# Feed-forward attention, last two head quads: scores of the fourth made beside the third's softmax, output projections spread between the two chains

## Chip, cores and metric

One Trainium2 chip, one core of it. The metric is the device time of one execution in microseconds (us). Shown are three plain executions and one profiled one.

## What is computed

A cross attention over 16 sequences of 128 rows is added to `x`; then a routed feed-forward layer works on the 256 rows (of 2048) that a router picks. Only that second layer is touched by the change:

```python
h = _rms_norm(x, ln1_w)                      # 256 picked rows x 512
q = (h @ wq + bq).reshape(S, 16, 128)        # rope is applied to q and kk
kk, v = ...                                  # 8 heads each, repeated to 16
att = softmax(where(causal, q.kk / sqrt(128), -max))
x1 = x + (att @ v).reshape(S, 2048) @ wo
h2 = _rms_norm(x1, ln2_w)
processed = x1 + silu(h2 @ w_gate) * (h2 @ w_up) @ w_down
gate = sigmoid(sel_scores)
output = hidden.at[picked].set(gate * processed + (1 - gate) * x)
```

## The kernel before

Every engine runs a program of its own, in the order in which it is written; semaphores tie them together. All matrix products are made of three passes (`product`): each operand is split into a high part, rounded to the matmul's fp32 format, and the rest, and high x high, high x low and low x high are added up in PSUM. So whatever PE is to multiply is first copied by ACT (the `_hi` copy) and then subtracted by DVE (the `_lo` part). For weights, ACT makes `wp_hi` (`split_high`) and POOL makes `wp_lo` (`split_low`, line 849); a weight piece is 512x512, and four slots hold pieces in turn (`wp_hi[n % NSLOT]`). Piece `n` may be split only when piece `n-4` has been used: `split_high` waits for `used_up[n - NSLOT]`. The pieces in question are 9, 10 and 11 (rows of `wo` for quads 1, 2, 3, in slots 1, 2, 3), 13 (`w_up`, first piece, slot 1) and 14 (`w_gate`, second piece, slot 2; in the code `P_MLP + 2`).

The 256 picked rows are two blocks of 128 (`j`). The 16 heads are four quads (`n`, `FQ = 4`) of four heads. For one quad the stages are: `turn_queries` (eight transposes of the roped queries), their hi and lo copies, `score_quad` (PE, three PSUM tiles), mask and maximum (DVE, lines 1581 and 1587), `Exp` head by head (ACT, line 1144), reciprocal (DVE, line 1595), normalisation (POOL, line 885), `turn_probs` (PE, 12 transposes, lines 1954 to 1959), hi and lo copies of the probabilities `fp`, `mix_quad` (PE, probabilities times values), hi and lo copies of the mixed heads `foT`, and `attend_out` (PE, products with a piece of `wo`, added up over all quads in the banks `b_xT` and `b_scores`' second half; per block j and quad it is 12 matmuls). `attn_done` counts finished groups of `attend_out`.

Up to quad 2 the query projections of the next quad stand between these stages on PE. For the last quad there are none left. PE's program from quad 2 on is written by hand:

```python
turn_queries(3); turn_probs(2); mix_quad(2); score_quad(3); attend_out(2)
turn_probs(3); mix_quad(3); attend_out(3)
```

with `attend_out(1)` just ahead of it, behind `score_quad(2)`. After that DVE adds the attention to the picked rows (`add_attention`, line 1610), ACT squares and sums the rows (`row_squares`, line 1044), POOL takes the inverse root (`row_rsqrt`, lines 855 and 858), DVE weighs the rows (`weigh`, line 1431), PE turns them (`turn_h`) and the MLP begins with `gate_rows(0, 0)`. On ACT `split_high(P_MLP + 2)` stands ahead of `row_squares`, and on POOL `split_low(P_MLP + 2)` stands ahead of `row_rsqrt`.

Two more steps matter. DVE forms the router's dot products `g_dot` (line 1603, both inputs in SBUF) between the reciprocals of quad 3 and the lo parts of its probabilities; the sigmoid from it (`g_exp` on ACT, line 1166; `g_one` and `gate` on DVE, lines 1619 and 1621) stands just ahead of the MLP's first `silu` step (line 1627).

Of the kernel before, what the change touches and what calls it, by code (L numbers as in the profile page):

```python
# [5 lines left out]
def xattn_then_routed_ffn(  # L6
# [48 lines left out]
    P = 128  # L55
# [89 lines left out]
    with ctx:  # L145
# [101 lines left out]
        with ExitStack() as st:  # L247
# [32 lines left out]
            f_max = sb_in(st, "f_max", [P, 8])  # L280
            f_sum = sb_in(st, "f_sum", [P, 8])
            f_inv = sb_in(st, "f_inv", [P, 8])
# [8 lines left out]
        base = [by_cos, by_sin]  # L291

# [13 lines left out]
        f_W = [b_xT, b_s2]  # L306

# [400 lines left out]
        def _(pool):  # L708
# [168 lines left out]

            for n in range(FQ):
# [4 lines left out]
                for i, (heads, col) in enumerate(SCORE_TILES):  # L883
                    pool.wait_ge(f_inverted, 3 * n + i + 1)
                    pool.tensor_tensor(
                        fs[i][:].rearrange("p (h t) -> p h t", h=heads),
                        fs[i][:].rearrange("p (h t) -> p h t", h=heads),
                        f_inv[:, col:col + heads].unsqueeze(2).to_broadcast([P, heads, W // heads]),
                        ALU.mult).then_inc(f_normed, 1)
# [22 lines left out]
        def _(act):  # L912
# [194 lines left out]
            def probs_high(n):  # L1107

                act.wait_ge(fp_turned, 3 * n + 1)
                wait(act, f_mixed, 2 * n)  # L1110
                copy(fp0_hi[:, 0:2, :].rearrange("p h t -> p (h t)"), f_T[:]).then_inc(fp_hi_done, 1)
                act.wait_ge(fp_turned, 3 * n + 2)
                copy(fp0_hi[:, 2:4, :].rearrange("p h t -> p (h t)"), f_T2[:]).then_inc(fp_hi_done, 1)
                act.wait_ge(fp_turned, 3 * n + 3)
                copy(fp1_hi[:].rearrange("p h t -> p (h t)"), f_S[:]).then_inc(fp_hi_done, 1)

            def mixed_high(n):
                for g in range(2):
                    act.wait_ge(f_mixed, 2 * n + g + 1)

                    wait(act, attn_done, NJ * n)
                    copy(foT_hi[:, 2 * g:2 * g + 2, :].rearrange("p h t -> p (h t)"),
                         (f_O, f_T)[g][:]).then_inc(fo_hi_done, 1)

            for n in range(FQ):
                for j in range(NJ):
# [3 lines left out]
                    copy(fqT_hi[:, j].rearrange("p h t -> p (h t)"), (f_T, f_T2)[j][:]  # L1130
                         ).then_inc(fq_hi_done, 1)
                if n > 0:
                    probs_high(n - 1)
                if n < FQ - 1:
                    split_high(split_early(n))
# [4 lines left out]
                for i, (heads, col) in enumerate(SCORE_TILES):  # L1140
                    width = W // heads
                    act.wait_ge(f_maxed, 3 * n + i + 1)
                    for h in range(heads):
                        e = act.activation(fs[i][:, h * width:(h + 1) * width],
                                           fs[i][:, h * width:(h + 1) * width], ACT.Exp,
                                           bias=f_max[:, col + h:col + h + 1],
                                           accum_out=f_sum[:, col + h:col + h + 1])
                    e.then_inc(f_exped, 1)
                if n == FQ - 1:
                    split_high(split_early(n))  # L1150
# [14 lines left out]
            act.wait_ge(g_dotted, NJ)  # L1165
            act.activation(g_exp[:], g_dot[:], ACT.Exp, scale=-1.0).then_inc(g_exped, 1)
# [17 lines left out]
        def _(dve):  # L1184
# [356 lines left out]

            def probs_low(n):
                for i, (hi, lo, bank) in enumerate((
                        (fp0_hi[:, 0:2, :], fp0_lo[:, 0:2, :], f_T),
                        (fp0_hi[:, 2:4, :], fp0_lo[:, 2:4, :], f_T2),
                        (fp1_hi[:], fp1_lo[:], f_S))):
                    dve.wait_ge(fp_hi_done, 3 * n + i + 1)
                    low(lo.rearrange("p h t -> p (h t)"), bank[:],
                        hi.rearrange("p h t -> p (h t)")).then_inc(fp_lo_done, 1)

            def mixed_low(n):
                for g in range(2):
                    dve.wait_ge(fo_hi_done, 2 * n + g + 1)
                    low(foT_lo[:, 2 * g:2 * g + 2, :].rearrange("p h t -> p (h t)"), (f_O, f_T)[g][:],
# [547 lines left out]
```

## Time and profile before

| what | us |
|---|---|
| median of 3 executions (873.81 to 878.23) | 876.07 |
| the profiled execution | 879.73 |
| its span, first to last instruction | 878.0 |
| PE busy / DVE busy / ACT busy / POOL busy | 820.9 / 577.5 / 474.0 / 464.0 |
| mean granted TensorE clock, as a share of full speed | 0.977 |

Busy time is an average over stages. The quads of the feed-forward attention run from about 717 to 796 us of the span, the MLP from 800 us to the end; what this change touches lies between 757 and 815 us. A row of the timeline gives the start, the duration, the engine, the line, the operation with output and inputs, and in brackets how long the engine sat idle before it and what released it. A matmul's duration includes its way through the array: back to back ones start every 0.23 us (512 columns) and overlap.

### The profile page before, as it was taken

To read this page: it belongs to the slowest core of one execution; us is meant where nothing else is said; L and a number is where in the kernel's file an instruction comes from. 1 tells how busy PE (TensorE), PEld (TensorE's weight loads), DVE (VectorE), ACT (ScalarE), POOL (GpSimd) and SP (SyncE) were. 2 spreads that over 40 slices of the span, in tenths; PEclk is the share of its full clock that TensorE was granted. 3 is DMA by queue.
4 is the path that set the end of the run, shared out by engine and by line. 5 is a ranking of instruction groups with operands and counts; after the bars stand their busy time and mean duration, and the time that the engine had idled before them with its cause. 6 is when DMAs were issued, how large, how long until landed. Compare 5 with 4: busy or idle time off the path is not lost. (4 is left out here: it accounts for less than half of the span.)

```text
span 878.0 us, 14307 instructions
## 1 busy us (share of the span) xinstructions
PE 820.9 (93%) x4216; PEld 683.7 (78%) x4216; DVE 577.5 (66%) x1049; ACT 474.0 (54%) x1620; POOL 464.0 (53%) x485
## 2 busy tenths in 40 slices
PE   6999958999999999999999999999987799978997
PEld 4888836888888888888888888888875677766786
DVE  4454445677777777777777777777677588663513
ACT  4555534565566566566566566566554256553431
POOL 2333324555555555555555555555557196644980
PEclk9999997999999999999999999999998699999999
DMA  6566654011111111111111111111024565303520
GB/s 206 202 203 204 202 180 135 13 61 36 48 60 36 48 60 36 48 60 36 48 60 36 48 60 36 48 60 36 24 90 140 213 182 178 118 29 117 192 97 24
DMA packets 49287, 81.37 MB, mean 93 GB/s; under 512 B 4144, under 2 KB 12464, under 8 KB 49264
## 3 DMA queue, kind: packets, MB, share of 16 engines
q1 hardware_dynamic: 48688, 79.25, 27.5%
q0 software_dynamic: 576, 1.84, 0.6%
q8 instruction: 12, 0.20, 0.1%
q14 instruction: 11, 0.09, 0.0%
HBM read 63.77 MB, written 17.30 MB: 92 GB/s over the span
## 5 line engine op out<-in xcount | busy, mean ns | idle before, releaser
L1002 ACT ACTIVATE sq_junk<-q_row 128x128 bf16<-128x128 f32 x256 | 76.0, 298 | 159.6 <-DVE q_row L1256 159.6
L849 POOL TENSOR_TENSOR wp_lo<-raw,wp_hi 128x2048 fp32r<-128x2048 f32 (+1 forms) x24 | 105.0, 4385 | 45.3 <-ACT wp_hi L914 45.2
L1010 ACT ACTIVATE p_row<-s_row,neg_max 128x128 f32<-128x128 f32 x256 | 99.9, 392 | 37.0 <-DVE neg_max L1277 36.4
L1656 PE MATMUL b_y<-wo_hi,oT_hi 128*128 128x512 f32 x256 | 107.1, 419 | 1.0 <-DVE oT_lo L1187 1.0
L1656 PE MATMUL b_q<-wq_hi,xT_hi 128*128 128x512 f32 x252 | 105.6, 419 | 2.2 <-DVE k_row L1210 2.2
L780 POOL TENSOR_TENSOR p_row<-p_row,p_inv 128x512 f32<-128x512 f32 x64 | 66.6, 1041 | 66.7 <-DVE p_inv L1286 66.7
L1658 PE MATMUL b_y<-wo_hi,oT_lo 128*128 128x512 f32 x256 | 101.7, 397 | 0.0
L1657 PE MATMUL b_y<-wo_lo,oT_hi 128*128 128x512 f32 x256 | 101.6, 397 | 0.0
L1658 PE MATMUL b_q<-wq_hi,xT_lo 128*128 128x512 f32 x252 | 99.7, 396 | 0.0
L1657 PE MATMUL b_q<-wq_lo,xT_hi 128*128 128x512 f32 x252 | 99.6, 395 | 0.0
L738 POOL TENSOR_TENSOR q_rs<-q_ss,eps_head 128x4 f32<-128x4 f32 x64 | 12.7, 199 | 153.8 <-ACT sq_junk L1002 153.8
L1256 DVE TENSOR_TENSOR q_row<-b_q,bq_row 128x512 f32<-128x512 f32 x63 | 43.6, 692 | 40.7 <-PE b_q L1658 40.6
L1743 PE MATMUL b_scores<-kT,qT_hi 128*128 128x256 f32 x256 | 64.8, 285 | 5.6 <-DVE qT_lo L1261 5.5
L776 POOL TENSOR_TENSOR q_nrm<-q_row,q_rs 128x512 f32<-128x512 f32 x64 | 66.6, 1040 | 6.1 <-POOL q_rs L740 2.2
L740 POOL TENSOR_TENSOR q_rs<-q_rs,half 128x4 f32<-128x4 f32 x64 | 64.9, 1013 | 5.0
L1744 PE MATMUL b_scores<-kT,qT_lo 128*128 128x256 f32 x256 | 64.8, 285 | 0.0
L914 ACT ACTIVATE wp_hi<-raw 128x2048 fp32r<-128x2048 f32 x24 | 45.9, 1915 | 30.6 <-PE b_y L1658 15.8
L1187 DVE TENSOR_TENSOR oT_lo<-b_o,oT_hi 128x512 fp32r<-128x512 f32 x64 | 43.7, 683 | 21.3 <-ACT oT_hi L914 20.0
L1658 PEld LDWEIGHTS b_y<-wo_hi,oT_lo 128*128 128x128 f32 x256 | 48.5, 189 | 11.8
L1743 PEld LDWEIGHTS b_scores<-kT,qT_hi 128*128 128x128 f32 x256 | 49.1, 192 | 10.3 <-DVE qT_lo L1261 6.8
L1267 DVE TENSOR_TENSOR s_row<-b_scores,mask 128x512 f32<-128x512 f32 x64 | 44.3, 692 | 19.0 <-PE b_scores L1744 19.0
L1658 PEld LDWEIGHTS b_q<-wq_hi,xT_lo 128*128 128x128 f32 x252 | 48.0, 191 | 11.0
(298 smaller groups left out, 2266.0 us busy)
## 6 DMA issues: line engine op xcount, KB each, us to landing
cx<-in_ctx_dram SPq DMA_DIRECT2D x16, 256.0 KB, 2.6
wq_raw<-in_L_xattn_Wq_dram SPq DMA_DIRECT2D x16, 256.0 KB, 2.8
wo_raw<-in_L_xattn_Wo_dram SPq DMA_DIRECT2D x16, 256.0 KB, 3.1
v_store<-v_out SPq DMA_DIRECT2D x16, 256.0 KB, 3.3
k_store<-k_out SPq DMA_DIRECT2D x16, 256.0 KB, 2.0
xr<-in_x_dram SPq DMA_DIRECT2D x16, 256.0 KB, 2.7
k_raw<-k_store SPq DMA_DIRECT2D x16, 256.0 KB, 2.6
v_raw<-v_store SPq DMA_DIRECT2D x16, 256.0 KB, 2.8
```

The costliest lines, as they stand in the source:

```text
L740: pool.tensor_tensor(dst, dst, half[:, 0:dst.shape[1]], ALU.pow).then_inc(rooted, 1)
L776: pool.tensor_tensor(q_nrm[:], q_row[:], per_head(q_rs, HD), ALU.mult).then_inc(q_normed, 1)
L780: pool.tensor_tensor(p_row[:], p_row[:], per_head(p_inv, S), ALU.mult).then_inc(p_normed, 1)
L849: pool.tensor_tensor(wp_lo[n % NSLOT][:, part, :], raw[RAW_OF[n]][:, part, :], wp_hi[n % NSLOT][:, part, :].bitcast(fp32), ALU.subtract).t ...
L914: return act.activation(dst, src, ACT.Copy)
L1002: sq = act.activation(sq_junk[:, h, :], q_row[:, h, :], ACT.Square, accum_out=q_ss[:, h:h + 1])
L1010: e = act.activation(p_row[:, h, :], s_row[:, h, :], ACT.Exp, bias=neg_max[:, h:h + 1], accum_out=p_sum[:, h:h + 1])
L1656: pe.matmul(dst, left[0], right[0], start=start, stop=False)
L1657: pe.matmul(dst, left[0], right[1], start=False, stop=False)
L1658: return pe.matmul(dst, left[1], right[0], start=False, stop=stop)
L1743: pe.matmul(b_scores[:, h, :], qT_hi[:, hs], keys, start=True, stop=False)
L1744: last = pe.matmul(b_scores[:, h, :], qT_lo[:, hs], keys, start=False, stop=True)
```

## The change

The scores of quad 3 are made on PE ahead of `turn_probs(2)`. To have room, quad 3 gets its own banks (`b_q`, `b_y`, `b_o` for queries and scores) and its own SBUF tiles for the scores (`proj[0]`, `proj[1]`, `by_cos` in place of `fs`), the statistics get two halves, and the mixed heads of quad 2 go into `hT` in place of `foT`. Since `by_cos` now holds scores, POOL's gather into it waits for the transposes of quad 3. The output projections are spread: block 0 of quad 1 ahead of the scores of quad 3, block 1 behind them; block 0 of quad 2 between the transposes and the mixing of quad 3; block 1 of quad 2 in two halves around block 0 of quad 3. The count that frees a weight slot follows that order. The sigmoid of the router moves ahead of the MLP on ACT and DVE.

```diff
+        def scores_of(n):
+            return (proj[0], proj[1], by_cos) if n == FQ - 1 else fs
+
+        def mixed_of(n):
...
+                     for t in (hT_hi, hT_lo)] if n == FQ - 2 else [foT_hi[:], foT_lo[:]]
...
+        def query_banks(n):
+            return (b_q, b_y) if n == FQ - 1 else (f_T, f_T2)
+
+        def score_banks(n):
+            return (b_q, b_y, f_O) if n == FQ - 1 else (f_S, f_T2, f_T)
+
+        def prob_banks(n):
+            return (b_q, b_y, f_S) if n == FQ - 1 else (f_T, f_T2, f_S)
...
+        OUTPUTS = [(n, j) for n in range(FQ - 2) for j in range(NJ)]
+        OUTPUTS += [(FQ - 2, 0), (FQ - 1, 0), (FQ - 2, 1), (FQ - 1, 1)]
+
+        def outputs_until(n, j):
+            return OUTPUTS.index((n, j)) + 1
...
-            used_up[p_wo(n)] = (attn_done, NJ * (n + 1))
+            used_up[p_wo(n)] = (attn_done, outputs_until(n, NJ - 1))
...
             pool.wait_ge(f_roped, NJ * (FK + FQ))
+            pool.wait_ge(fp_turned, 3 * FQ)
...
+            for n in range(FQ - 1):
+                queries_high(n)
...
+                if n == FQ - 2:
+                    queries_high(FQ - 1)
+                score_exps(n)
...
+            score_exps(FQ - 1)
+            probs_high(FQ - 2)
+            mixed_high(FQ - 2)
+            split_high(split_early(FQ - 1))
             probs_high(FQ - 1)
             mixed_high(FQ - 1)
+            act.wait_ge(g_dotted, NJ)
+            act.activation(g_exp[:], g_dot[:], ACT.Exp, scale=-1.0).then_inc(g_exped, 1)
             split_high(P_MLP + 2)
             for j in range(NJ):
                 act.wait_ge(x2_made, j + 1)
                 row_squares(NJ + j, x2_row[j][:])
+            act.wait_ge(attn_done, outputs_until(FQ - 2, NJ - 1))
...
+            mask_scores(FQ - 2, 0)
+            mask_scores(FQ - 2, 1)
+            queries_low(FQ - 1)
+            mask_scores(FQ - 2, 2)
+            invert(FQ - 2, 0)
+            invert(FQ - 2, 1)
+            mask_scores(FQ - 1, 0)
+            invert(FQ - 2, 2)
+            mask_scores(FQ - 1, 1)
+            mask_scores(FQ - 1, 2)
+            invert(FQ - 1, 0)
+            probs_low(FQ - 2)
+            invert(FQ - 1, 1)
+            invert(FQ - 1, 2)
+            mixed_low(FQ - 2)
...
             probs_low(FQ - 1)
             mixed_low(FQ - 1)
+            dve.wait_ge(g_exped, 1)
+            dve.tensor_scalar(g_one[:], g_exp[:], 1.0, None, ALU.add).then_inc(g_made, 1)
...
+            turn_queries(FQ - 1)
+            attend_out(FQ - 3, 0)
+            score_quad(FQ - 1)
+            attend_out(FQ - 3, 1)
+            turn_probs(FQ - 2)
+            mix_quad(FQ - 2)
             turn_probs(FQ - 1)
+            attend_out(FQ - 2, 0)
             mix_quad(FQ - 1)
-            attend_out(FQ - 1)
+            attend_out(FQ - 2, 1, range(0, 2))
+            attend_out(FQ - 1, 0)
+            attend_out(FQ - 2, 1, range(2, QUAD))
+            attend_out(FQ - 1, 1)
```

Three places in the built programs show it. First PE, from the transposes of the last queries to the last output projection; of every block its first instruction stands here (`wp_hi1`, `wp_hi2` and `wp_hi3` are the slots with `wo` for quads 1, 2 and 3). Before:

```order
L1663 MATMUL b_pT<-ident,turned1 128x128 [waits f_masked,f_roped]
L1954 MATMUL b_qT<-ident,fs0 128x128 [waits fq_lo_done,f_normed]
L1656 MATMUL b_o<-fp0_hi,fv_hi 128x512 [waits fo_lo_done,fp_lo_done]
L1656 MATMUL b_scores<-fkT_hi,fqT_hi 128x128 [waits fp_lo_done,fq_lo_done]
L1656 MATMUL b_xT<-wp_hi2,foT_hi 128x512 [waits fo_lo_done,piece_lo_pool]
L1954 MATMUL b_qT<-ident,fs0 128x128 [waits f_normed]
L1656 MATMUL b_xT<-wp_hi3,foT_hi 128x512 [waits fo_lo_done,piece_lo_pool]
```

and with the change:

```order
L1732 MATMUL b_y<-ident,turned1 128x128 [waits f_roped]
L1725 MATMUL b_xT<-wp_hi1,foT_hi 128x512 [waits fo_lo_done,piece_lo_pool]
L1725 MATMUL b_q<-fkT_hi,fqT_hi 128x128 [waits fq_lo_done]
L1725 MATMUL b_scores<-wp_hi1,foT_hi 128x512 [waits fo_lo_done,piece_lo_pool]
L2028 MATMUL b_qT<-ident,fs0 128x128 [waits fq_lo_done,f_normed]
L1725 MATMUL b_o<-fp0_hi,fv_hi 128x512 [waits fo_lo_done,f_masked,fp_lo_done]
L2028 MATMUL b_q<-ident,proj0 128x128 [waits fp_lo_done,f_normed]
L1725 MATMUL b_xT<-wp_hi2,hT_hi 128x512 [waits fo_lo_done,piece_lo_pool]
L1725 MATMUL b_scores<-wp_hi2,hT_hi 128x512 [waits fo_lo_done,piece_lo_pool]
L1725 MATMUL b_xT<-wp_hi3,foT_hi 128x512 [waits fo_lo_done,piece_lo_pool]
L1725 MATMUL b_scores<-wp_hi3,foT_hi 128x512 [waits fo_lo_done,piece_lo_pool]
```

The scores of quad 3 (`b_q<-fkT_hi`) now come ahead of the transposed probabilities of quad 2 (`b_qT<-ident,fs0`), and both blocks of `wo` for quad 2 (`wp_hi2`) come late; the second half of its block 1 is the last but one group of all.

Second ACT, from the split of piece 13 (`wp_hi1<-raw2`) to the first `row_squares` (`hn_row0,f_ss`); piece 14 is `wp_hi2<-raw0`. Before:

```order
L914 ACTIVATE wp_hi1<-raw2 128x2048 [waits attn_done,raw_loaded2]
L914 ACTIVATE fp0_hi<-b_qT 128x512 [waits f_mixed,fp_turned]
L914 ACTIVATE foT_hi<-b_qT 128x512 [waits attn_done,f_mixed]
L914 ACTIVATE wp_hi2<-raw0 128x2048 [waits attn_done,raw_loaded0]
L1044 ACTIVATE hn_row0,f_ss<-x2_row0 128x512 [waits x2_made]
```

and with the change:

```order
L941 ACTIVATE hT_hi<-b_qT 128x512 [waits f_mixed]
L941 ACTIVATE wp_hi1<-raw2 128x2048 [waits attn_done,raw_loaded2]
L941 ACTIVATE fp0_hi<-b_q 128x512 [waits f_mixed,fp_turned]
L941 ACTIVATE foT_hi<-b_qT 128x512 [waits attn_done,f_mixed]
L1196 ACTIVATE g_exp<-g_dot 128x2 [waits g_dotted]
L941 ACTIVATE wp_hi2<-raw0 128x2048 [waits attn_done,raw_loaded0]
L1071 ACTIVATE hn_row0,f_ss<-x2_row0 128x512 [waits x2_made]
```

The split of piece 13 has moved from behind the `Exp`s of quad 3 to behind the mixed heads of quad 2. The split of piece 14 stands where it stood, ahead of `row_squares`; what moved is the event that it waits for: `attn_done` was 6 (both blocks of quad 2, then ahead of quad 3's transposes) and is 7 now, which the second half of block 1 of quad 2 raises.

Third DVE, around the dot products `g_dot` (`fp0_lo`: lo parts of probabilities). Before:

```order
L1587 TENSOR_REDUCE f_max<-fs2 128x2 [waits f_masked]
L1595 RECIPROCAL f_inv<-f_sum 128x4 [waits f_exped]
L1595 RECIPROCAL f_inv<-f_sum 128x2 [waits f_exped] x2
L1603 ISA x2_row0,g_dot<-h_sel0,wr2_row 128x512 [waits f_rows_loaded]
L1603 ISA x2_row1,g_dot<-h_sel1,wr2_row 128x512
L1187 TENSOR_TENSOR fp0_lo<-b_qT,fp0_hi 128x512 [waits fp_hi_done]
```

and with the change:

```order
L1617 TENSOR_REDUCE f_max<-by_cos 128x2 [waits f_masked]
L1623 RECIPROCAL f_inv<-f_sum 128x4 [waits f_exped]
L1227 TENSOR_TENSOR fp0_lo<-b_qT,fp0_hi 128x512 [waits fp_hi_done]
L1623 RECIPROCAL f_inv<-f_sum 128x2 [waits f_exped] x2
L1227 TENSOR_TENSOR hT_lo<-b_qT,hT_hi 128x512 [waits fo_hi_done]
L1672 ISA x2_row0,g_dot<-h_sel0,wr2_row 128x512 [waits f_rows_loaded]
L1672 ISA x2_row1,g_dot<-h_sel1,wr2_row 128x512
L1227 TENSOR_TENSOR fp0_lo<-b_q,fp0_hi 128x512 [waits fp_hi_done]
```

Two reciprocals of quad 3 now stand behind the lo parts of quad 2's probabilities, and the dot products stand behind the mixed heads of quad 2.

## Rows read from the trace of the kernel before

**Rows 1.** Busy time by stretch: stretch, length, then PE, PEld, DVE, ACT, POOL busy (instructions), clock, DMA

```profile
757.90:760.70 2.80, 2.80 (x27) 2.80 (x26) 2.73 (x5) 2.40 (x2) 1.49 (x2) 1.00 0.07 16
777.10:782.60 5.50, 5.50 (x26) 4.31 (x24) 4.50 (x11) 5.35 (x17) 2.59 (x3) 1.00 0.00 0
815.00:860.00 45.00, 45.00 (x212) 37.50 (x211) 16.82 (x22) 18.28 (x19) 35.45 (x8) 1.00 0.40 140
```

**Rows 2.** Who PE waited for from 735 us on: total, times, longest

```profile
PE b_o L1656 <- DVE fp_lo L1187: 5.2, 4, 1.7
...
PE b_qT L1663 <- DVE hn_row L1431: 1.7, 1, 1.7
...
PE b_q L1656 <- DVE turned L1627: 0.9, 1, 0.9
```

**Rows 3.** The chain of work that ended last, pieces between 766 and 798 us

```profile
766.31 0.45 PE b_qT L1663 x4
...
769.52 0.61 ACT fp_hi L914
...
772.09 0.50 PE b_o L1656
...
789.71 1.91 ACT wp_hi L914
791.70 4.61 POOL wp_lo L849
...
797.26 0.75 DVE hn_row L1431
```

**Rows 4.** Timeline of PE: first matmul of quad 3's scores; turned rows; start of the MLP

```profile
774.31 0.22 PE L1656 MATMUL b_scores<-fkT_hi,fqT_hi 128*128 128x128 f32 x1
...
798.07 0.66 PE L1663 MATMUL b_qT<-ident,hn_row 128*128 128x128 f32 x4 [1.67 <-DVE hn_row L1431]
800.73 0.77 PE L1656 MATMUL b_q<-wp_hi,hT_hi 128*128 128x512 f32 x1 [2.00 <-DVE hT_lo L1187]
...
803.42 0.57 PE L1656 MATMUL b_q<-wp_hi,hT_hi 128*128 128x512 f32 x1
```

**Rows 5.** Timeline of DVE and ACT: mixed heads of quad 2, softmax of quad 3, piece 13

```profile
775.14 0.69 DVE L1187 TENSOR_TENSOR foT_lo<-b_qT,foT_hi 128x512 fp32r<-128x512 f32 x1 [0.36 <-ACT foT_hi L914]
777.12 0.68 DVE L1581 SCALAR_TENSOR_TENSOR fs<-b_pT,causal 128x512 f32<-128x512 f32 x1
778.45 0.68 DVE L1581 SCALAR_TENSOR_TENSOR fs<-b_qT,causal 128x512 f32<-128x512 f32 x1
...
774.51 0.60 ACT L914 ACTIVATE foT_hi<-b_qT 128x512 fp32r<-128x512 f32 x1 [0.45 <-PE b_qT L1658]
779.88 0.51 ACT L1144 ACTIVATE fs<-fs,f_max 128x256 f32<-128x256 f32 x1
780.88 1.90 ACT L914 ACTIVATE wp_hi<-raw 128x2048 fp32r<-128x2048 f32 x1
```

**Rows 6.** Timeline of POOL: normalisations of quads 2 and 3, and piece 13

```profile
765.17 3.03 POOL L885 TENSOR_TENSOR fs<-fs,f_inv 128x512 f32<-128x512 f32 x3
780.01 3.48 POOL L885 TENSOR_TENSOR fs<-fs,f_inv 128x512 f32<-128x512 f32 x3 [11.82 <-DVE f_inv L1595]
783.46 5.01 POOL L849 TENSOR_TENSOR wp_lo<-raw,wp_hi 128x2048 fp32r<-128x2048 f32 x1
```

**Rows 7.** Groups by line and shape: the two kinds of dot product: total us, mean ns

```profile
L1309 DVE CUSTOM_DVE_ANT_0 dot_junk<-h_row,wr_row 128x512 bf16<-128x512 f32 x16 | 11.1, 692 | 0.6
...
L1603 DVE CUSTOM_DVE_ANT_0 x_row<-h_sel,wr_row 128x512 f32<-128x512 f32 x2 | 3.0, 1510 | 0.0
```

**Rows 8.** Timeline of DVE at the MLP's first silu step

```profile
809.12 4.60 DVE L1619 TENSOR_SCALAR g_one<-g_exp 128x2 f32<-128x2 f32 x1 [2.17 <-ACT g_exp L1166]
```

**Rows 9.** Timeline of PE after two waits, an earlier place: first slow and first faster matmul

```profile
695.41 0.79 PE L1656 MATMUL b_y<-wp_hi,hT_hi 128*128 128x512 f32 x1 [2.28 <-DVE hT_lo L1187]
...
701.12 0.52 PE L1657 MATMUL b_scores<-wp_lo,hT_hi 128*128 128x512 f32 x1
```

More of the change, by code:

```diff
@@ L1105, in _, with queries_high @@
                     split_high(NSLOT + o)
[L1107 to L1125, printed above, removed]
+            def queries_high(n):
                 for j in range(NJ):
@@ L1129, in _, with probs_high, mixed_high, score_exps @@
                     wait(act, f_scored, 3 * n)
-                    copy(fqT_hi[:, j].rearrange("p h t -> p (h t)"), (f_T, f_T2)[j][:]
+                    copy(fqT_hi[:, j].rearrange("p h t -> p (h t)"), query_banks(n)[j][:]
                          ).then_inc(fq_hi_done, 1)
+            def probs_high(n):
+                places = (fp0_hi[:, 0:2, :], fp0_hi[:, 2:4, :], fp1_hi[:])
+                for i in range(3):
+                    act.wait_ge(fp_turned, 3 * n + i + 1)
+                    if i == 0:
+                        wait(act, f_mixed, 2 * n)
+                    copy(places[i].rearrange("p h t -> p (h t)"), prob_banks(n)[i][:]).then_inc(fp_hi_done, 1)
+            def mixed_high(n):
+                hi, lo = mixed_of(n)
+                for g in range(2):
+                    act.wait_ge(f_mixed, 2 * n + g + 1)
+                    if n == FQ - 1:
+                        act.wait_ge(attn_done, outputs_until(FQ - 3, NJ - 1))
+                    elif n < FQ - 2:
+                        wait(act, attn_done, NJ * n)
+                    copy(hi[:, 2 * g:2 * g + 2, :].rearrange("p h t -> p (h t)"),
+                         (f_O, f_T)[g][:]).then_inc(fo_hi_done, 1)
+            def score_exps(n):
+                for i, (heads, col) in enumerate(SCORE_TILES):
+                    width = W // heads
+                    tile_ = scores_of(n)[i]
+                    act.wait_ge(f_maxed, 3 * n + i + 1)
+                    for h in range(heads):
+                        e = act.activation(tile_[:, h * width:(h + 1) * width],
+                                           tile_[:, h * width:(h + 1) * width], ACT.Exp,
+                                           bias=f_max[:, n % 2, col + h:col + h + 1],
+                                           accum_out=f_sum[:, n % 2, col + h:col + h + 1])
+                    e.then_inc(f_exped, 1)
+            for n in range(FQ - 1):
+                queries_high(n)
                 if n > 0:
                     probs_high(n - 1)
-                if n < FQ - 1:
-                    split_high(split_early(n))
+                split_high(split_early(n))
                 if n > 0:
@@ L1139, in _ @@
                     split_high(piece)
[L1140 to L1150, printed above, removed]
+                if n == FQ - 2:
+                    queries_high(FQ - 1)
+                score_exps(n)
                 if n == 0:
@@ L1556, in mixed_low, with mask_scores @@
                         ).then_inc(fo_lo_done, 1)
-            for n in range(FQ):
-                if n < FQ - 1:
-                    o = PROJECTIONS.index(("q", n + 1))
+            def mask_scores(n, i):
+                heads, col = SCORE_TILES[i]
+                width = W // heads
+                tile_ = scores_of(n)[i][:].rearrange("p (h t) -> p h t", h=heads)
+                dve.wait_ge(f_scored, 3 * n + i + 1)
+                if n < FQ - 1:
+                    wait(dve, fp_turned, 3 * n)
+                dve.scalar_tensor_tensor(
+                    tile_, score_banks(n)[i][:].rearrange("p (h t) -> p h t", h=heads), SCALE,
+                    causal[:, 2 * P - width:2 * P].unsqueeze(1).to_broadcast([P, heads, width]),
+                    ALU.mult, ALU.add).then_inc(f_masked, 1)
+                dve.wait_ge(f_masked, 3 * n + i + 1)
+                dve.tensor_reduce(f_max[:, n % 2, col:col + heads], tile_,
+                                  AX.X, ALU.max, negate=True).then_inc(f_maxed, 1)
@@ L1561, in _, with invert @@
+            def invert(n, i):
+                heads, col = SCORE_TILES[i]
+                dve.wait_ge(f_exped, 3 * n + i + 1)
+                dve.reciprocal(f_inv[:, n % 2, col:col + heads],
+                               f_sum[:, n % 2, col:col + heads]).then_inc(f_inverted, 1)
+            for n in range(FQ - 2):
+                o = PROJECTIONS.index(("q", n + 1))
                 if n == 0:
                     take_rows(o, 0)
-                for j in range(NJ):
-                    dve.wait_ge(fq_hi_done, NJ * n + j + 1)
-                    low(fqT_lo[:, j].rearrange("p h t -> p (h t)"), (f_T, f_T2)[j][:],
-                        fqT_hi[:, j].rearrange("p h t -> p (h t)")).then_inc(fq_lo_done, 1)
@@ L1592, in _ @@
                     take_rows(PROJECTIONS.index(("v", 1)), 1)
-                for i, (heads, col) in enumerate(SCORE_TILES):
-                    dve.wait_ge(f_exped, 3 * n + i + 1)
-                    dve.reciprocal(f_inv[:, col:col + heads],
-                                   f_sum[:, col:col + heads]).then_inc(f_inverted, 1)
+                for i in range(3):
+                    invert(n, i)
                 if n == 0:
```

143 lines of the change are left out of this document (75 added, 68 removed).

## The prediction

> **What bounds the kernel now.** I read the view of who waited for whom first, on PE, since PE is the engine that is busy 93% of the span. From 735 us on it waits for little, and all of it lies at the end of the attention: 5.2 us in four waits for the lo parts of probabilities, and 1.7 us for the normalised row ahead of the MLP [rows 2]. The busy times by stretch show the same from the other side: in the scores of a quad (2.80 of 2.80 us) and in the output projection of a quad (5.50 of 5.50) PE has no gap, and none in the MLP from 815 to 860 us (45.00 of 45.00) [rows 1]. So a microsecond taken off the start of the MLP comes off the end of the kernel, and one added there is added.
>
> Then I read the chain that ended last, at the point where the MLP starts, because that tells what sets this start. It is not the last output projection. PE is done with it at 796.40 (798.07 less the 1.67 it then sat idle) [rows 4]. The chain goes through ACT's split of weight piece 14 at 789.71, POOL's lo part of it at 791.70 for 4.61 us, and only then the inverse root and the weighed row at 797.26 [rows 3]. POOL works in order, and this 4.61 us piece stands ahead of the inverse root. From the start of ACT's split to the turned row on PE it is 798.07 - 789.71 = **8.36 us**, whatever PE does meanwhile.
>
> **The change, part by part.** The work on PE is the same, 0 matmuls added or removed; what moves are its gaps. Up to the end of quad 2's scores at 760.70 nothing moves. From there I lay PE's new order out, on the clock of the profiled execution, with four transposes at 0.45 us [rows 3], a block of output projection at 5.50 / 2 = 2.75, scores at 2.80 [rows 1], and a mixing at 774.31 - 772.09 = 2.22 [rows 3, 4].
>
> - *First stretch, no gap.* Queries of quad 3 (0.9), block 0 of quad 1 (2.75), scores of quad 3 (2.80, done at 767.15), block 1 of quad 1 (2.75): 769.9. POOL has quad 2's probabilities normalised at 765.17 + 3.03 = 768.2 [rows 6]; DVE now puts the queries' two lo parts ahead of the last mask, and a mask of quad 3 ahead of the last reciprocal, some 2 us, but POOL is busy with piece 12 until 765.17 anyway, so I move this by at most 0.2. Transposes of quad 2 (1.35): 771.25.
> - *Quad 2's probabilities.* ACT's hi copies now stand behind all `Exp`s of quad 3. DVE takes the first mask of quad 3 at about 765.8 and the others 778.45 - 777.12 = 1.33 apart [rows 5], with one reciprocal between: the last maximum is there at 769.95. The last two `Exp`s take 780.88 - 779.88 = 1.0 [rows 5], so the copies start at 770.95. From that start to the mixing it is 772.09 - 769.52 = 2.57 [rows 3]: mixing at 773.5. PE sits idle 2.25, where it was idle 1.7.
> - *Quad 2 out.* Mixing until 775.75, transposes of quad 3 until 777.1 (two of its reciprocals stand behind quad 2's lo parts on DVE and are done at 773.5, POOL follows with two of the three tiles, 2.0 us, at 775.6: just in time). The mixed heads are ready 775.14 + 0.69 - 772.09 = 3.74 after a mixing starts [rows 3, 5], at 777.25. Block 0 of quad 2 until 780.05.
> - *Quad 3's probabilities.* The second hi copy of quad 2's mixed heads starts 774.51 - 772.09 = 2.42 into the mixing [rows 3, 5], at 775.9; ACT then splits piece 13, which used to lie behind quad 3's `Exp`s, 1.90 us [rows 5], until 778.3. The copies of quad 3 start there, and mixing 2.57 later at 780.9, if DVE is free by 778.9. It has the two dot products first, from 777.2 on.
> - *The dot products.* They took 1.51 us each; the same kind of product elsewhere took 0.69 [rows 7]. Beside them POOL's three normalisations took 3.48 in place of 3.03, and piece 13 took 5.01 [rows 6] in place of 4.61 [rows 3]: each lost about 0.45 while DVE lost 0.8. So they lengthened each other. Now they stand at 777.2 to 778.7, where POOL has nothing until ACT hands it piece 13 at 778.4. I take 0.73 each; with 1.51 each DVE would be free at 780.2 and mixing starts 1.2 us later. The Trainium skill, "SBUF — State Buffer", section "Who interferes with whom", says that a VectorE instruction with two SBUF inputs and a GpSimd instruction that reads SBUF exclude each other, the second waiting out the first; by it the sum would be the one with 0.73, by the row at face value 1.2 us more. The trace agrees: 1.51 is 0.69 and most of one 1.0 us normalisation.
> - *Quad 3 out.* Mixing 780.9 to 783.1, heads ready at 784.65. Half a block of quad 2 (1.38) fits in between. Block 0 of quad 3 until 787.4, the other half block until 788.8, block 1 of quad 3 until 791.5. PE is thus done **4.9 us earlier** than at 796.40.
> - *What takes it back.* ACT may split piece 14 only when slot 2 is free. That was long so when ACT came to it at 789.71 [rows 3]. Now ACT is free at 784.5, but the slot is used until the second half block of quad 2, 788.8, and the count rises some 0.2 after the next matmul could start: the split begins at 789.0. The piece on POOL and the inverse root stand behind it as before: 789.0 + 8.36 = 797.35 for the turned row, against 798.07. **Of 4.9 us, 0.7 are left.**
> - *The sigmoid.* DVE's `g_one`, two columns, took 4.60 us beside a POOL piece that began at the same moment [rows 8], and PE then waited 0.9 for the first `silu` step [rows 2]. Moved to about 785, where POOL only issues gathers, it stands on no path: **-0.9**.
> - *The clock.* PE will sit idle 797.35 - 791.7 = 5.7 us ahead of the turned row, then 2.0. Before it was 1.67 and 2.00, and the MLP started at half speed (1.2 GHz) for 803.42 - 800.73 = 2.7 us [rows 4]. After two longer idle times it was 701.12 - 695.41 = 5.7 us [rows 9]. In these 2.7 us six matmuls started, 0.45 each, against 5.50 / 24 = 0.23 [rows 1], so each microsecond at half speed costs about half of itself. Between 0 and 3.0 / 2 = 1.5; I take **+0.5**, since the idle stretch is longer and the place where speed comes back differs from one start to the next.
> - Wider statistics, other PSUM banks and other SBUF tiles are the same instructions with other addresses: nothing. POOL's extra wait ahead of its gathers ends at 777, while POOL is on piece 13 until 783: nothing; were it exposed, the gathers are needed only in the MLP.
>
> Sum: -0.7 - 0.9 + 0.5 = **-1.1 us** against 879.73, the profiled execution. That is 3.7 above the median; the same difference on the median of 876.07 gives **875.0**. Less than 0.5% (4.4 us) either way can't be told from no change here; the three executions alone spread over 4.4.
>
> **The rivals.**
> *The output projections set the start.* If piece 14 did not hold up the inverse root, the turned row would follow PE's last projection at 791.5 and the gain would be 6.6 + 0.9 = 7.5: about 868.5. For it: PE's order does end 4.9 us earlier. Against it: the order on ACT and POOL still has piece 14 first, and the count it waits for is raised by the last but one group.
> *The dot product meets piece 13 on POOL.* If the second dot product is issued after POOL has begun piece 13, DVE may stand until that ends, as `g_one` did for 4.60 us [rows 8]. The point is sharp: the dot product is issued at 777.95, the piece starts at 778.4, 0.45 us later, and both hang on the same copy of ACT. If it falls the other way, DVE is free at 778.4 + 4.61 + 0.55 = 783.55 in place of 778.9, mixing of quad 3 and all behind it is 4.6 later: -1.1 + 4.6 = +3.5, and with the clock at its upper bound +4.5: 879.6 to 880.6, slower than before.
> *The clock.* If the long idle time keeps the MLP's whole first two tiles slow, 24 matmuls at 0.22 more less the 6 slow ones of before, it costs 4.0 in place of 0.5: 878.5.
>
> **How the numbers follow.** The forecast, with what lies within a few microseconds of it, gets 0.62; the first rival, with any other way in which the early end of PE counts, 0.14; the dot product 0.10; the clock 0.10; the rest, spread, 0.04. The forecast's own bounds are -0.7 - 0.9 + 0 - 1 (links of the chain that are shorter than I laid them) = -2.6 and -0.7 + 1.2 - 0.9 + 1.5 = +1.1, so 873.5 to 877.2, with some 2 us for the median of few executions. To hold 8 of 10 the range must reach over the clock and towards the second rival: 871 to 880. Faster by over 0.5%: the first rival and a bit of scatter, 0.15. Slower by over 0.5%: the upper half of the second rival and the rest, 0.10. Within: 0.75.
>
> **What would show it.** Right: ACT's split of piece 14 starts right behind a wait for PE, near 789; POOL's piece follows it and the inverse root that; PE idles some 5 us ahead of the turned row; scores of quad 3 stand ahead of the transposes of quad 2 with no gap between; `g_one` takes well under 1 us; the dot products take 0.7 each. Wrong: the turned row comes close behind the last projection, or a dot product lasts over 4 us, or PE waits elsewhere in the MLP.

## The result: a little slower, and the profile after

| | before | after |
|---|---|---|
| median, us (20 runs each) | 878.16 (873.81 to 882.39) | 880.34 (876.77 to 883.25) |
| profiled execution: span, time, us | 878.0, 879.73 | 876.9, 878.74 |
| PE busy, us | 820.9 | 821.0 |

The ratio is **1.0028, 95% interval 1.0017 to 1.0039**: 0.0028 x 878 = 2.5 us slower, where the prediction had 1.1 faster. That is within the 0.5% either way to which the prediction gave 0.75, but it is clear of no change. Before is 2.1 us above the median that the prediction began with, so the differences are compared, not the times.

The profiled execution of after came to the first score of quad 2 at 753.81, 4.1 us earlier than that of before [rows 1]: the program up to there is the same, and single executions differ by that much (753.81 to 758.53 in the twelve traces of this document). So 4.1 is added to a time of after wherever it is compared with one of before ("aligned").

Busy time of PE by stretch in after (stretch, length, PE, PEld, DVE, ACT and POOL busy, clock, DMA share, GB/s), the scores of quad 2 and a place in the MLP:

```profile
753.80:756.60 2.80, 2.80 (x27) 2.80 (x26) 2.74 (x5) 2.40 (x2) 1.48 (x2) 1.00 0.15 19
...
829.20:833.60 4.40, 4.39 (x13) 3.49 (x14) 1.87 (x3) 0.00 (x0) 3.93 (x1) 0.63 0.64 233
```

The first row answers to the first of [rows 1] and is the same work at the same speed. The second lies where before had 45 us of MLP at a clock of 1.00 without a gap: now 4.4 us at 0.63, part of them at the lower of the two levels of the clock.

Who PE waited for from 735 us on, in after:

```profile
PE b_qT L1732 <- DVE hn_row L1471: 5.6, 1, 5.6
PE b_o L1725 <- DVE fp_lo L1227: 3.5, 3, 2.2
PE b_q L1725 <- DVE turned L1696: 2.7, 1, 2.7
PE b_q L1725 <- DVE hT_lo L1227: 1.6, 1, 1.6
```

Against [rows 2], the wait for the normalised row grew from 1.7 to 5.6, as forecast (5.7). The wait for `turned`, 0.9 before, was to go and is 2.7 now. It is not the same wait: before, it stood at the first `silu` step of the MLP; now there is none there, and 2.7 at the second. PE's timeline in after shows where:

```profile
769.41 0.50 PE L1725 MATMUL b_o<-fp_hi,fv_hi 128*128 128x512 f32 x1 [2.18 <-DVE fp_lo L1227]
776.67 0.50 PE L1725 MATMUL b_o<-fp_hi,fv_hi 128*128 128x512 f32 x1 [0.40 <-DVE fp_lo L1227]
...
793.29 1.11 PE L1732 MATMUL b_qT<-ident,hn_row 128*128 128x128 f32 x4 [5.64 <-DVE hn_row L1471]
795.97 0.76 PE L1725 MATMUL b_q<-wp_hi,hT_hi 128*128 128x512 f32 x1 [1.56 <-DVE hT_lo L1227]
...
829.21 0.47 PE L1725 MATMUL b_q<-wp_hi,hT_hi 128*128 128x512 f32 x1 [2.72 <-DVE turned L1696]
...
830.96 0.63 PE L1725 MATMUL b_q<-wp_hi,hT_hi 128*128 128x512 f32 x1
831.38 0.63 PE L1726 MATMUL b_q<-wp_lo,hT_hi 128*128 128x512 f32 x1
```

The turned row stands at 793.29 + 4.1 = 797.39 aligned (798.07 before, 797.35 forecast), the MLP at 800.07 against 800.73 [rows 4]. **Up to there the change gains 0.7 us, as forecast.** From the start of the MLP to the last step on DVE it is then 76.7 us, against 73.05 before: 3.7 lost. Less the 0.7, 3.0 in these two executions, near the 2.5 measured. The loss is in the row at 829.21: a gap of 2.72 us, and behind it matmuls that start 0.42 apart (half speed, 1.2 GHz) in place of 0.23, for some eight of them: about 1.6 us more. The first 12 matmuls of the MLP, partly at half speed too, took 0.3 us longer than before, and the wait of 0.9 at the first `silu` is gone: 2.7 + 1.6 + 0.3 - 0.9 = 3.7. The place lies behind the stretch of 757 to 815 us that the change was taken to touch.

The chain that ended last, in after, says what made PE wait:

```profile
785.02 1.93 ACT wp_hi L941
787.02 4.50 POOL wp_lo L872
...
792.48 0.75 DVE hn_row L1471
...
818.45 10.01 DVE h_sel L1712 x2
828.46 0.61 DVE turned L1696
829.21 0.47 PE b_q L1725
```

The upper rows are the piece 14 of [rows 3]. Below stands a step that the prediction never mentions: two instructions of VectorE on `h_sel` with 10.01 us between them. This is the **gating step**, `attn_row * gate + base`, two `scalar_tensor_tensor` with two big SBUF inputs each. It stands in the loop over the MLP at `m == 0`, ahead of the second `silu` step. VectorE in after, in order of time:

```profile
773.05 0.68 DVE L1672 CUSTOM_DVE_ANT_0 x_row<-h_sel,wr_row 128x512 f32<-128x512 f32 x1
...
780.33 0.16 DVE L1677 TENSOR_SCALAR g_one<-g_exp 128x2 f32<-128x2 f32 x1
...
818.45 5.03 DVE L1712 SCALAR_TENSOR_TENSOR h_sel<-h_sel,gate,by_cos 128x512 f32<-128x512 f32 x1
823.40 5.06 DVE L1712 SCALAR_TENSOR_TENSOR h_sel<-h_sel,gate,by_sin 128x512 f32<-128x512 f32 x1
828.38 0.68 DVE L1696 SCALAR_TENSOR_TENSOR turned<-proj,b_q 128x512 f32<-128x512 f32 x1
```

and the same step in before:

```profile
824.12 3.84 DVE L1643 SCALAR_TENSOR_TENSOR h_sel<-h_sel,gate,by_cos 128x512 f32<-128x512 f32 x1
827.88 0.74 DVE L1643 SCALAR_TENSOR_TENSOR h_sel<-h_sel,gate,by_sin 128x512 f32<-128x512 f32 x1
```

The second instruction took 0.74 us before and 5.06 after, on the same data. What changed is what POOL does at that moment. POOL in before:

```profile
809.08 18.33 POOL L849 TENSOR_TENSOR wp_lo<-raw,wp_hi 128x2048 fp32r<-128x2048 f32 x4 [8.79 <-ACT wp_hi L914]
828.81 4.63 POOL L849 TENSOR_TENSOR wp_lo<-raw,wp_hi 128x2048 fp32r<-128x2048 f32 x1 [1.40 <-ACT wp_hi L914]
```

and in after:

```profile
804.57 18.37 POOL L872 TENSOR_TENSOR wp_lo<-raw,wp_hi 128x2048 fp32r<-128x2048 f32 x4 [9.07 <-ACT wp_hi L941]
823.14 4.78 POOL L872 TENSOR_TENSOR wp_lo<-raw,wp_hi 128x2048 fp32r<-128x2048 f32 x1 [0.20 <-ACT wp_hi L941]
```

In both, the first gating instruction meets the fourth of four weight pieces that lie back to back, and ends 0.54 to 0.55 us after that piece does (827.96 against 827.41, 823.48 against 822.94). Before, POOL then had a gap of 1.40 us, and the second instruction ended at 828.62, **0.19 us before POOL's next piece**; it had begun 0.93 us before that piece (827.88 against 828.81). After, the gap is 0.20 us, the piece is there first (823.14 against 823.40), and the second instruction stands until the piece ends at 827.92.

The gap shrank because two chains moved against each other. POOL's next piece waits for ACT's split, and that for PE's up rows (this is ACT's row in before, then in after):

```profile
826.81 1.92 ACT L914 ACTIVATE wp_hi<-raw 128x2048 fp32r<-128x2048 f32 x1 [2.47 <-PE b_o L1658]
```

```profile
821.14 1.92 ACT L941 ACTIVATE wp_hi<-raw 128x2048 fp32r<-128x2048 f32 x1 [2.47 <-PE b_o L1727]
```

From the start of the MLP this is 26.08 us before and 25.17 after: 0.91 earlier, mostly the wait at the first `silu` (0.85) that the change removed. POOL's four pieces end 0.29 later (26.68 and 26.97), as they begin later behind the slower start of the MLP. 1.40 - 0.91 - 0.29 = 0.20: a shift of 1.20 us between the two chains, more than the 0.93 by which the second instruction had come first.

### The profile page after: what moved, and what is told of

The parts are those of the page before. It is cut to its first block and busy times, and to the rows that moved or that the text cites. A ratio compares the mean times of both kernels' runs of the same rounds, so it can differ in the third digit from the quotient of the medians.

```text
span 876.9 us, 14307 instructions
## 1 busy us (share of the span) xinstructions
PE 821.0 (94%) x4216; PEld 683.6 (78%) x4216; DVE 575.3 (66%) x1049; ACT 474.6 (54%) x1620; POOL 462.4 (53%) x485
## 5 line engine op out<-in xcount | busy, mean ns | idle before, releaser
L1725 PEld LDWEIGHTS b_q<-wq_hi,xT_hi 128*128 128x128 f32 x252 | 48.3, 192 | 10.5 <-issue 2.4
```

The source lines that it names most:

```text
L1725: pe.matmul(dst, left[0], right[0], start=start, stop=False)
```

## The experiments

The theory: the change gains what was forecast, and its early sigmoid brings the gating step to meet one GpSimd piece more, which costs more than all that was gained. The rival: the new order of the attention costs it, by its long idle time of PE, by the clock or otherwise. No run leaves out any of the computation. All ratios are to the kernel before; us are (ratio - 1) x 878; the last three columns are read from the traces.

| run | ratio, 95% interval | us | second gating instruction, us | POOL's gap, us | wait at the second `silu`, us |
|---|---|---|---|---|---|
| before | 1 | 0 | 0.74 | 1.40 | none |
| the change | 1.0028 (1.0017 to 1.0039) | +2.5 | 5.06 | 0.20 | 2.7 |
| change, gating late | 0.9979 (0.9957 to 1.0001) | -1.8 | 0.74 | 0.20 | none |
| change, gating early | 0.9995 (0.9972 to 1.0018) | -0.4 | 0.75 | 0.21 | none |
| change, sigmoid back | 0.9994 (0.9973 to 1.0016) | -0.5 | 0.74 | 1.43 | none |
| before, sigmoid early | 1.0031 (1.0011 to 1.0051) | +2.7 | 5.07 | 0.25 | 2.7 |
| before, gating late | 1.0005 (0.9983 to 1.0026) | +0.4 | 0.75 | 1.39 | none |
| before, sigmoid early, gating late | 0.9983 (0.9965 to 1.0001) | -1.5 | 0.74 | 0.26 | none |
| change, piece 14 late | 0.9968 (0.9952 to 0.9983) | -2.8 | 5.06 | 0.23 | 2.7 |
| change, piece 14 and gating late | 0.9918 (0.9897 to 0.9938) | -7.2 | 0.75 | 0.20 | none |
| before, piece 14 and gating late | 0.9989 (0.9973 to 1.0005) | -1.0 | 0.74 | 1.37 | none |
| change, both moves, and piece 14 behind the second weighing | 0.9916 (0.9886 to 0.9945) | -7.4 | 0.75 | 0.20 | none |

POOL's gap is 0.20 to 0.26 in every run with the early sigmoid and 1.37 to 1.43 in every run with the late one, whatever else differs. Only where the gating step stands at its old place does the second gating instruction meet that gap.

**The change, gating late.**

```diff
-                if m == 0:
+                if m == FI - 2:
```

> The changed kernel, with VectorE's gating step of the attention rows (the two scalar_tensor_tensor on h_sel, two SBUF inputs each) moved from the first silu step of the MLP to the last but one. Theory (the gating step now meets GpSimd's weight pieces, and PE waits for the silu behind it): the two gating instructions at their old place took 10.1 us and cost PE a wait of 2.7 us and 1.7 us of half speed; at the new place GpSimd has no piece left, they take about 0.75 us each, the wait and the half speed go, and the kernel is 4.4 us faster than the change: about 1.9 us faster than before, ratio 0.998. Rival (the new order of the attention, its long idle time of PE or its clock, costs the 2.5 us): the ratio stays 1.003, whatever the gating instructions take.

Measured: 0.9979, 0.0049 x 878 = 4.3 us under the change; its interval leaves out the rival's 1.003. The gating step and PE's waits in this run:

```profile
L1712 DVE SCALAR_TENSOR_TENSOR h_sel<-h_sel,gate,by_cos x1: 743/743/743, 855.6 to 855.6; 128x512 f32<-128x512 f32 x1
L1712 DVE SCALAR_TENSOR_TENSOR h_sel<-h_sel,gate,by_sin x1: 744/744/744, 856.3 to 856.3; 128x512 f32<-128x512 f32 x1
```

```profile
PE b_qT L1732 <- DVE hn_row L1471: 5.6, 1, 5.6
PE b_o L1725 <- DVE fp_lo L1227: 3.9, 3, 2.2
PE b_q L1725 <- DVE hT_lo L1227: 1.6, 1, 1.6
```

The wait of 5.6 us ahead of the turned row is all there, so it is not what makes the change slower than before; the wait of 2.7 is gone.

**Before, gating late**, the same edit on the kernel before, as a control.

> The kernel before, with the gating step moved to the last but one silu step, as a control. Theory: the gating instructions took 3.84 and 0.74 us there and no PE wait came of it, so 0 us, ratio 0.999 to 1.001. Rival (the late place is worth several microseconds by itself, whatever the change did, for instance since it frees GpSimd's weight pieces): 1 us faster or more, ratio below 0.9985; then the run of the change with the late gating does not speak for the theory.

Measured: 1.0005. The interval (0.9983 to 1.0026) shows no gain from the late place by itself, where no wait of PE came of the gating step.

**The change, gating early.** The whole gating step stands behind the second `h_low`, ahead of the loop, its waits with it:

```diff
             h_low(NJ + 1)
+            dve.wait_ge(attn_copied, NJ)
+            dve.wait_ge(g_made, 2)
+            dve.wait_ge(gathered_base, 16 * NJ)
+            for j in range(NJ):
+                dve.scalar_tensor_tensor(attn_row[j][:], attn_row[j][:], gate[:, j:j + 1], base[j][:],
...
```

> The changed kernel with the gating step not later but earlier: on VectorE right behind the second h_low, ahead of the first silu step of the MLP, where GpSimd has been idle since the inverse roots and takes its next piece only about 8.6 us after the start of the MLP. Theory (what costs is meeting a GpSimd piece, not the place in the MLP): both gating instructions take about 0.75 us, end some 0.4 us ahead of GpSimd's piece, the wait of 2.7 us goes: as with the gating late, 4.4 us faster than the change, ratio to before 0.998. Rival (it is the distance from the busy first steps of the MLP that helps, or less work on VectorE there): 1.003, or slower still, since 1.5 us more stand ahead of the first silu step.

Both instructions pass ahead of POOL's pieces:

```profile
803.48 0.75 DVE L1695 SCALAR_TENSOR_TENSOR h_sel<-h_sel,gate,by_cos 128x512 f32<-128x512 f32 x1 [0.29 <-ACT h_sel L941]
804.15 0.75 DVE L1695 SCALAR_TENSOR_TENSOR h_sel<-h_sel,gate,by_sin 128x512 f32<-128x512 f32 x1
...
805.33 18.36 POOL L872 TENSOR_TENSOR wp_lo<-raw,wp_hi 128x2048 fp32r<-128x2048 f32 x4 [9.13 <-ACT wp_hi L941]
```

Measured: 0.9995, and the wait of 2.7 is gone. The interval leaves out the rival's 1.003 and holds the 0.998 expected, though the middle lies 1.3 us short of it. So it is the meeting that costs, not the place in the MLP.

**The change, sigmoid back**: the sigmoid where before had it, everything else as changed.

```diff
             split_high(P_MLP + 3)
+            act.wait_ge(g_dotted, NJ)
+            act.activation(g_exp[:], g_dot[:], ACT.Exp, scale=-1.0).then_inc(g_exped, 1)
...
             h_low(NJ + 1)
+            dve.wait_ge(g_exped, 1)
+            dve.tensor_scalar(g_one[:], g_exp[:], 1.0, None, ALU.add).then_inc(g_made, 1)
...
```

> The changed kernel, with the sigmoid alone put back where it was before (exponential on ACT behind the split of piece 15, the two small VectorE steps behind the second h_low). Theory (the 0.9 us that PE gained there closed GpSimd's gap from 1.4 to 0.2 us, and the second gating instruction lost its place in it): g_one takes some 4.6 us again, PE waits some 0.9 us at the first silu step, GpSimd's gap is over 1 us again, the second gating instruction takes about 0.75 us and not 5.06, no wait of 2.7 us: 0.7 us faster than before less up to 0.3 for the clock, ratio 0.9993. Rival (the order of the attention costs it): 1.003 or, with the 0.9 us given back, 1.004.

VectorE and POOL in this run:

```profile
806.09 4.60 DVE L1688 TENSOR_SCALAR g_one<-g_exp 128x2 f32<-128x2 f32 x1 [2.17 <-ACT g_exp L1206]
...
821.05 3.85 DVE L1712 SCALAR_TENSOR_TENSOR h_sel<-h_sel,gate,by_cos 128x512 f32<-128x512 f32 x1
824.83 0.74 DVE L1712 SCALAR_TENSOR_TENSOR h_sel<-h_sel,gate,by_sin 128x512 f32<-128x512 f32 x1
```

```profile
825.78 4.61 POOL L872 TENSOR_TENSOR wp_lo<-raw,wp_hi 128x2048 fp32r<-128x2048 f32 x1 [1.43 <-ACT wp_hi L941]
```

With `g_one` slow again, POOL's gap is 1.43, the second instruction 0.74, and the time 0.9994: **a wait of 0.9 us put back makes the kernel some 3 us faster.**

**Before, sigmoid early**, the reverse: that one part of the change alone.

> The kernel before, with the sigmoid alone moved ahead of the MLP as the change has it, and no other part of the change. Theory: PE's wait of 0.9 us at the first silu step goes, GpSimd's gap closes, the second gating instruction waits out one more piece (about 5 us in place of 0.74), and the kernel is 2.5 to 3.6 us slower than before: ratio 1.003 to 1.004, though PE waits less. Rival: this part is worth what the prediction gave it, 0.9 us faster, ratio 0.999, and the loss is in the order of the attention.

```profile
788.50 0.16 DVE L1608 TENSOR_SCALAR g_one<-g_exp 128x2 f32<-128x2 f32 x1
...
821.29 4.99 DVE L1643 SCALAR_TENSOR_TENSOR h_sel<-h_sel,gate,by_cos 128x512 f32<-128x512 f32 x1
826.20 5.07 DVE L1643 SCALAR_TENSOR_TENSOR h_sel<-h_sel,gate,by_sin 128x512 f32<-128x512 f32 x1
```

POOL's piece, PE's two waits, and PE's busy time with the granted clock (here the stretch, PE, clock, DMA share, GB/s):

```profile
825.98 4.74 POOL L849 TENSOR_TENSOR wp_lo<-raw,wp_hi 128x2048 fp32r<-128x2048 f32 x1 [0.25 <-ACT wp_hi L914]
...
796.22 0.66 PE L1663 MATMUL b_qT<-ident,hn_row 128*128 128x128 f32 x4 [1.77 <-DVE hn_row L1431]
832.01 0.47 PE L1656 MATMUL b_q<-wp_hi,hT_hi 128*128 128x512 f32 x1 [2.69 <-DVE turned L1627]
...
826.87:834.87 8.00, 5.31 (x24) 1.00 0.76 245
```

Measured: 1.0031, as much as the whole change loses, with the attention in its old order and PE's idle time ahead of the turned row at 1.77 us. The rival falls here. In this execution the clock stayed at 1.00 behind the gap of 2.7, so the 1.6 us of half speed seen in after is not in every execution: of the three traces with this gap, two have half speed behind it (after and the change with piece 14 late).

**Before, sigmoid early and gating late.**

> The kernel before, with the sigmoid early and the gating step late, and nothing else. Theory (the early sigmoid alone is worth its 0.9 us as soon as no gating step stands among GpSimd's pieces): PE's wait of 0.9 us goes, no other comes, ratio 0.999. Rival (the early sigmoid loses by something else than the gating step): 1.003, as with the sigmoid alone.

Measured: 0.9983, so the early sigmoid no longer loses as soon as the gating step is out of the way; between this run and the one above lie 4.2 us. PE's wait of 0.9 is gone in the trace and no other came. That this is a gain in time is not shown: the interval (0.9965 to 1.0001) reaches no change.

**The change, piece 14 and gating late.** This asks what the rest of the change could give; the gating step is moved as above.

```diff
-            split_low(P_MLP + 2)
             for j in range(NJ):
                 row_rsqrt(NJ + j)
+            split_low(P_MLP + 2)
...
-            split_high(P_MLP + 2)
             for j in range(NJ):
                 act.wait_ge(x2_made, j + 1)
                 row_squares(NJ + j, x2_row[j][:])
+                if j == 0:
+                    split_high(P_MLP + 2)
```

> The changed kernel with the gating step at the last but one silu step and, besides, weight piece 14 moved behind the inverse roots: ACT splits it between the squares of the two rows, GpSimd makes its lo part behind both inverse roots. Theory (the early end of the output projections is held back by piece 14 alone, and the gating step took the rest): PE, done with the projections some 4.9 us earlier than before, starts the MLP 4 to 5 us after their end, as the kernel before did (800.73 - 796.40 = 4.3), so 3.3 to 4.0 us earlier than the change; with 4.4 us for the gating step some 7.5 faster than the change, 5 faster than before: ratio 0.994. Rival (the new order of the attention gives nothing that can be had, or the idle time it makes is paid in the clock): as the change with the gating late, 0.998.

Measured: **0.9918, 7.2 us faster than before, more than the 5 expected.** PE has no gap ahead of the turned row:

```profile
789.06 0.60 PE L1733 MATMUL b_qT<-ident,hn_row 128*128 128x128 f32 x4
792.06 0.76 PE L1726 MATMUL b_q<-wp_hi,hT_hi 128*128 128x512 f32 x1 [2.40 <-DVE hT_lo L1228]
```

From the first score of quad 2 (754.62) to the start of the MLP (792.06) it is 37.4 us, against 42.8 before and 42.2 in the change. I had taken the 4.3 us that before needed from its last projection to the MLP; here it is 3.0, since the first row is weighed while the last projections still run.

**The change, piece 14 late**, gating at its old place.

> The changed kernel with weight piece 14 alone moved behind the inverse roots, the gating step at its old place. Theory: the MLP starts 3.3 to 4.0 us earlier than in the change; GpSimd's pieces of the MLP and PE's steps move with it together, so that GpSimd's gap stays at some 0.2 us, the gating step takes some 10 us and the wait of 2.7 us stays: 0.8 to 1.5 us faster than before, ratio 0.9985. Rival (the gating step collides only because the MLP starts late against the pieces): the second gating instruction takes 0.75 us, and the ratio is 0.994, as with the gating late.

Measured: 0.9968. The collision stays (5.06 us, a wait of 2.7), as expected, and the start of the MLP is again worth more than I had put down: 37.7 us behind the first score of quad 2, 4.5 earlier than in the change. In this execution the move also made a collision of its own. The second weighing stood beside piece 14 (794.39 on POOL), and PE, at full speed here, waited 1.7 us for it:

```profile
794.63 4.86 DVE L1472 SCALAR_TENSOR_TENSOR hn_row<-x_row,f_rs,ln_row 128x512 f32<-128x512 f32 x1
...
799.55 0.66 PE L1733 MATMUL b_pT<-ident,hn_row 128*128 128x128 f32 x4 [1.72 <-DVE hn_row L1472]
```

**Before, piece 14 and gating late.**

> The kernel before, with the same two moves (piece 14 behind the inverse roots, gating step late), without the change. Theory: here PE sat idle only 1.7 us between the last projection and the turned row, so piece 14 held back little: 0 to 1.2 us faster than before, ratio 0.9985 to 1.0; the 5 us of the run with both moves on the change then come from the change. Rival (they come from the two moves, and the change adds nothing): 0.994 here too.

Measured: 0.9989. So of the 7.2 us, some 6 need the change, and two things kept them back, piece 14 and the gating step. They are not the order of the attention alone, since this run has the late sigmoid as well, with PE's wait of 0.9. By the traces the start of the MLP lies 41.7 us behind the first score of quad 2 here and 37.4 with the change: 4.3 us for the order, and 0.9 for the sigmoid; what is left of the 6 is less than the intervals leave open.

**The change, both moves, and piece 14 behind the second weighing.** POOL waits with piece 14 for the second weighed row besides (`pool.wait_ge(hn_made, 2 * NJ)` ahead of `split_low(P_MLP + 2)`).

> The kernel with both moves on the change, with GpSimd besides waiting for the second weighed row before it starts piece 14. In the run with both moves the second weighing took 4.85 us, as it was issued 0.25 us after GpSimd had begun that piece. Theory (the same exclusion): it takes 0.75 us here, piece 14 starts some 1.1 us later and lies in the 4.75 us in which GpSimd had nothing; PE came to the second row some 4.7 us after the start of the MLP at half speed, so that most of it was hidden there and 1.7 us where PE ran at full speed: 0 to 1.7 us faster than with both moves, ratio to before 0.990 to 0.992. Rival (piece 14 is needed by PE as early as it came): slower than with both moves, 0.993 or more, with a new PE wait on the lo part of the weights.

Measured: 0.9916, not to be told from 0.9918. The second weighing took 4.85 us at 791.83 in the run with both moves and 0.74 here, so the exclusion is seen once more, but PE was busy with the first row meanwhile in the execution of the run with both moves.

## Why the prediction was wrong

- **The attention, up to the turned row: right.** Mixing of quad 2 waited 2.18 us (2.25 forecast); the dot products took 0.68 and 0.69 (0.73); the projections were done at 793.29 - 5.64 + 4.1 = 791.75 (791.5); ACT's split of piece 14 came right behind a wait for PE, at 785.02 + 4.1 = 789.12 (789.0); the turned row at 797.39 (797.35). Of the 4.65 us by which the projections ended earlier (796.40 against 791.75; 4.9 forecast), 0.7 were left. That piece 14 took the rest is shown by the runs with it late: there the MLP starts 4.5 to 4.7 us earlier than in the change.
- **The sigmoid: the step that failed.** The prediction gave it -0.9, as it "stands on no path". `g_one` did shrink from 4.60 [rows 8] to 0.16 us, and PE's wait at the first `silu` did go. But the term as a whole measured +2.7 us where it stood alone (before, sigmoid early; +1.0 to +4.5 by the interval). The sentence on which the sum rests, that "a microsecond taken off the start of the MLP comes off the end of the kernel", does not cover it. With piece 14 late the whole MLP starts 4.5 us earlier, POOL's gap stays (0.23), and the kernel is 5.3 us faster than the change. The 0.9 us, though, lies behind the start of the MLP, between PE and POOL: PE's up rows set when ACT splits the next piece, and so when POOL begins it, while POOL's four pieces ahead of it did not end earlier. The gap closed, and 2.7 us came back as a wait of PE, in after with 1.6 us of half speed behind it.
- The danger could be read from before. The first gating instruction took 3.84 us there, the second 0.74, and the second began only 0.93 us before POOL's next piece and ended 0.19 us before it. Against that margin a forecast shift of 0.9 is a toss-up, not nothing; the shift was 1.20, and 1.15 with the early sigmoid alone (the gap went from 1.40 to 0.25). The prediction priced `g_one` and the dot products, where the waits are seen, and not the third step of the kind, behind which PE did not wait yet. The row of the MLP without a gap (45.00 of 45.00) [rows 1] said that nothing waited, not that nothing was near. Nor do PE's waits all lie "at the end of the attention", as the prediction read them: the 0.9 at the first `silu` [rows 2] is in the MLP.
- **The rival that ended slower** had the right mechanism at the wrong place: it put the collision at the second dot product and piece 13, at 3.5 us slower. That one fell the good way, by little: the second dot product began at 773.66, 0.63 us ahead of POOL's piece at 774.29 (0.45 forecast), and ended at 773.66 + 0.69 = 774.35, as the piece began.
- **The clock: +0.5 can't be told apart.** In the first 4 us of the MLP the granted clock was 0.62 in before and 0.55 in the change; with the old order and the gating late it was 0.50, with piece 14 late 1.00. The first 12 matmuls of the MLP took 4.5, 4.6, 5.2 and 5.2 us in the traces with 5.6 and 1.6 us of idle time ahead, and 4.3, 4.4, 5.2 and 5.3 with 1.7 or 1.8 and 2.0. So single executions differ by about a microsecond, and no order by the length of the idle time is seen; 0.3 of the 0.5 us stands in the pair of before and after.
- **The output projections set the start**: wrong for this change, as argued, since piece 14 stood first; the runs with it late show that what the rival described is there to be had.

The rule that the prediction drew on fits the gating rows of every run. As the Trainium skill, "SBUF — State Buffer", section "Who interferes with whom", has it, a VectorE instruction with two SBUF inputs and a GpSimd instruction that reads SBUF exclude each other, and the order of issue decides who waits. The gating rows agree: the second instruction took 0.74 to 0.75 us with POOL idle or in a gap of 1.40 to 1.43, and 5.06 to 5.07 where the gap was 0.20 to 0.25.

## What to carry to other kernels

Where two engines exclude each other, list every instruction of the kind, not only those that are waited for now, and write beside each its margin, from its own start to the start of the other engine's next instruction; a change that shifts one chain against the other by more than the smallest margin can cost a whole instruction, whatever it gains by itself. Put such instructions where the other engine is idle for long (after its last piece), rather than in a gap that happens to fit. And when an earlier end is held back by one step that is queued ahead, as piece 14 here, move that step in the same change: by the traces the new order brought the start of the MLP forward by 4.3 us with that move and by 0.7 without. Then look for what the move itself now meets, as the second weighing met piece 14.

## What the runs showed of the hardware that was not expected

A VectorE instruction that waits for GpSimd got through at the end of the piece it met. With more pieces to follow back to back this is seen at `g_one` in before: it stood from 809.12 to 813.72 [rows 8], one piece of about 4.6 us, while POOL's row of four from 809.08 went on to 827.41. The first gating instruction in after, begun at 818.45, met the last piece of such a row (by quarters of the row, just behind its start) and ended 0.54 us after it. The next VectorE instruction, begun at 823.40, then lost to the piece that POOL had begun at 823.14 and waited that one out too. So two such instructions in a row, beside pieces 0.20 us apart, cost nearly two pieces: 10.01 us of VectorE for work that takes 1.5. Where between a gap of 0.25 and one of 1.40 us the second begins to pass was not tried.
